# Self-attention of a fused attention block: value products four key blocks at a time instead of two

## The chip, the cores and the metric

The kernel runs on one core of a Trainium2 chip. The metric is the device time of one execution in microseconds (us); the time before is a median of 3 runs, 1094.27 us (1092.45 to 1095.04). The engines run side by side, each through its own list of instructions, and wait for each other by semaphores: PE (TensorE, matmuls and their weight loads), DVE (VectorE), ACT (ScalarE), POOL (GpSimd) and SP, which issues transfers. Matmul results land in PSUM, eight banks of 128 x 512 floats, and DVE or ACT copies them out.

## The reference

All is in float32, for x of 4 batches x 512 tokens x 160 channels. First an adapter layer (8 heads of 20) is applied. Then comes a block with three parts: self-attention with 20 heads of 64 over 512 tokens, cross-attention with 77 context tokens, and a feed-forward layer. The change is in the self-attention:

```python
x = cross_attention(layer_norm(x, g1, be1), layer_norm(x, g1, be1), wq1, wk1, wv1, wo1, bo1) + x

def cross_attention(x, ctx, wq, wk, wv, wo, bo):
    q, k, v = ...                                     # projections, 20 heads of 64
    scores = jnp.einsum('bhnd,bhmd->bhnm', q, k) * SCALE
    attn = jax.nn.softmax(scores, axis=-1)
    out = jnp.einsum('bhnm,bhmd->bhnd', attn, v)
    out = out.transpose(0, 2, 1, 3).reshape(B, N, HEADS * DHEAD)
    return jnp.einsum('bnf,fe->bne', out, wo) + bo
```

## The kernel before

The self-attention (`selfattn`, from L280) handles two heads at a time, a pair j of 10 in each batch (64 + 64 rows fill the 128 partitions). A pair has four blocks of 128 queries or keys. A unit u = 4j + q is one such block, 40 in a batch, and the program of every engine is written out over double units d, 20 in a batch, two units in each. The order of the instructions on each engine is the order of the code; nothing reorders it but the waits.

For a unit PE makes the scores of both heads (L388, six matmuls for a unit, as the product is made of three parts for each head) into a double bank. DVE takes the negated row maxima (L577), ACT the exponentials with their sums (L505, two per unit), DVE the reciprocals (L581), POOL scales the probabilities (L645). When all four units of a pair are scaled, PE transposes them by key block (`turns`, L402: eight transposes for a unit, four for each head e into the bank `b_turn[e]`). DVE copies the bank of head 0 (L586) and ACT that of head 1 (L516) into the SBUF tile `turned`, which has two buffers, u % 2. Each bank is single: the transposes of the next unit wait until the copy of their bank is done (L400). Then PE makes the value products (`pv`, L415): for each key block k of a pair two matmuls, one per head, which the profile records as four; each has 64 columns of weights, 512 moving columns and accumulates over k = 0..3 in one bank, `b_out`. After the fourth ACT copies this to `att` (L511), and at the end of a batch PE projects it out (`project_out`, L422), and DVE adds it to x (L594).

PE's order in double unit d (L444 to L466): the value products of units 2d-2 and 2d-1; in an even d the value projection (L232 to L235) of the pair after the next; the norm's transposes in d = 11 and 13; the transposes of unit 2d; the key projection (even d) or query projection (odd d), L224 to L227; the transposes of unit 2d+1; the scores of units 2d+6 and 2d+7, which may belong to the next batch. Behind d = 19 come the value products of units 38 and 39 and the output projection; d = 0 has no value products.

ACT's order (L529 to L546): the rounding of the next norm's output in d = 15 (L198 to L201); the exponentials of units 2d+4 and 2d+5, those whose scores PE made at the end of the double unit before, with the norm's scaling between them in d = 11 and 13 (L181, L186); in an even d the copy of the attention output (L511); the copy of transposed unit 2d; the rounding of k or q (L497, L493); the copy of unit 2d+1. DVE's order (L613 to L633): both maxima, a reciprocal, the copy of v in an even d (L573), the copy of unit 2d, a reciprocal, the copy of unit 2d+1, the remainder of k or q (L568, L563), and the norm's statistics behind d = 6 (L135, L139) and its standardizing behind d = 7 (L153).

A copy into `turned` waits for the transposes and for the value products that read that buffer last, s_pv of unit u-2.

Of the kernel before, what the change touches and what calls it, by code (L numbers as in the profile page):

```python
# [25 lines left out]
B, S, D = 4, 512, 160  # L26
P = 128
QT = S // P
# [30 lines left out]
def over_batches(eng, body):  # L59

    for b in range(B):
        body(b, b < B - 1)
# [217 lines left out]
def selfattn(nc, block, x, ident, ln, next_ln, w_q, w_k, w_v, w_o, bias_o, banks):  # L280

    NU = NPAIR * QT
# [16 lines left out]
    with ExitStack() as ctx:  # L299
        sb = lambda n, s, d=F32: ctx.enter_context(nc.sbuf_tensor("sa_" + n, s, d))  # L300
# [2 lines left out]
        k_parts = sb("k_parts", [P, 2, 2, S], F32R)  # L303
        v = sb("v", [P, 3, QT, 2 * P])
        probs = sb("probs", [P, 2, 2, QT, S])
        turned = sb("turned", [P, 2, 2, S])
        att = sb("att", [P, NPAIR, S])
        negmax = sb("negmax", [P, RING, 2])
        total = sb("total", [P, RING, 2])
# [2 lines left out]
        b_scores, b_turn, b_out, b_proj = [banks.pair(0), banks.pair(2)], banks[4:6], banks[6], banks[7]  # L312
# [16 lines left out]
        s_evac = sig("turned_copied", NU, 2)  # L329
        s_evac_act = sig("turned_copied_act", NU, 2)  # L330
        s_pv = sig("pv_made", NU, 6 * QT)
# [5 lines left out]
        def following(b, more):  # L337

            return (ln, b + 1, b + 1) if more else (next_ln, b + 1, 0)

        def wait_turned_copied(eng, b, u, e):

            s = s_evac_act if e == 1 else s_evac
            eng.wait_ge(s.sem, s.at(b, u))


        @block.tensor
        def _(pe):
            for s in (s_q, s_k, s_v, s_scores, s_turn, s_pv, s_o):
                pe.sem_inc(s.sem, s.credit)  # L350

            def project_q(b, j, bank=b_proj):
                ln.project(pe, bank, w_q, j * P).then_inc(s_q.sem, 1)

            def project_k(b, j, bank=b_proj):
                ln.project(pe, bank, w_k, j * P).then_inc(s_k.sem, 1)

            def project_v(b, j, bank=b_proj):
                for t in range(2):
                    last = ln.project_tokens(pe, bank[:, t * 2 * P:(t + 1) * 2 * P], w_v, j // 2 * 2 * P, j % 2 * 2 + t, 2 * P)  # L360
                last.then_inc(s_v.sem, 1)

            def next_q(b, j):
                if j == 0:
                    ln.ready(pe, b)
                pe.wait_ge(s_klo.sem, s_klo.at(b, j - 1))
                project_q(b, j)

            def next_v(b, j):
                pe.wait_ge(s_qlo.sem, s_qlo.at(b, j))  # L370
                project_v(b, j)

            def next_k(b, j):
                pe.wait_ge(s_vsb.sem, s_vsb.at(b, j))
                project_k(b, j)

            def scores(b, u):

                j, q = divmod(u, QT)
                if q == 0:  # L380
                    pe.wait_ge(s_qlo.sem, s_qlo.at(b, j))
                    pe.wait_ge(s_klo.sem, s_klo.at(b, j))
                pe.wait_ge(s_exp.sem, s_exp.at(b, 2 * u - 3))
                bank = b_scores[u % 2]
                for i, (a, c) in enumerate(((0, 0), (1, 0), (0, 1))):
                    for e in range(2):
                        rows = slice(e * HD, (e + 1) * HD)
                        last = pe.matmul(bank[:, e, :], q_parts[rows, j % 2, a, q * P:(q + 1) * P], k_parts[rows, j % 2, c, :],  # L388
                                         start=(i == 0), stop=(i == 2))
                last.then_inc(s_scores.sem, 1)  # L390

            def turns(b, u):

                j, k = divmod(u, QT)
                if k == 0:
                    pe.wait_ge(s_norm.sem, s_norm.at(b, 2 * QT * j + 2 * QT - 1))
                for e in range(2):
                    if u == 0:
                        pe.wait_ge(s_x.sem, s_x.at(b, e - 2))
                    wait_turned_copied(pe, b, u - 1, e)  # L400
                    for q in range(QT):
                        last = pe.transpose(b_turn[e][:, q * P:(q + 1) * P], probs[:, j % 2, e, q, k * P:(k + 1) * P], ident[:])  # L402
                    last.then_inc(s_turn.sem, 1)

            def pv(b, u):

                j, k = divmod(u, QT)
                for e in range(2):
                    wait_turned_copied(pe, b, u, e)
                if k == 0:  # L410
                    pe.wait_ge(s_vsb.sem, s_vsb.at(b, j | 1))
                    pe.wait_ge(s_att.sem, s_att.at(b, j - 1))
                for e in range(2):
                    c = j % 2 * P + e * HD
                    last = pe.matmul(b_out[e * HD:(e + 1) * HD, :], v[:, V_BUF[j // 2], k, c:c + HD],  # L415
                                     turned[:, u % 2, e, :], start=(k == 0), stop=(k == QT - 1))
                last.then_inc(s_pv.sem, 1)

            def project_out(q, first, end):

                for j in range(first, end):
                    last = pe.matmul(b_turn[q // 2][:, q % 2 * D:(q % 2 + 1) * D], att[:, j, q * P:(q + 1) * P],  # L422
                                     w_o[:, j, :], start=(j == 0), stop=(j == NPAIR - 1))
                return last

            ln.ready(pe, 0)
            project_q(0, 0, b_proj)
            project_k(0, 0, b_out)
            project_q(0, 1, b_turn[0])
            project_k(0, 1, b_turn[1])  # L430
            scores(0, 0)
            scores(0, 1)
            project_v(0, 0, b_proj)
            pe.wait_ge(s_klo.sem, s_klo.at(0, 0))
            project_v(0, 1, b_out)
            for u in range(2, 2 * LEAD):
                scores(0, u)
            project_q(0, 2, b_turn[0])
            for u in range(2 * LEAD, 2 * LEAD + 2):
                scores(0, u)  # L440
            pe.wait_ge(s_qlo.sem, s_qlo.at(0, 2))

            def batch(b, more):
                for d in range(ND):  # L444
                    norm, _, nb = following(b, more)
                    if d >= 1:
                        pv(b, 2 * d - 2)
                        pv(b, 2 * d - 1)
                    if d % 2 == 0:
                        over(next_v, b, d // 2 + 2, NPAIR, more)  # L450
                    if d == TURN_MAIN:
                        norm.turn_main(pe, nb, ident, b_proj, lambda: pe.wait_ge(s_klo.sem, s_klo.at(b, d // 2 + 2)))
                    if d == TURN_TAIL:
                        norm.turn_tail(pe, nb, ident, b_proj, lambda: pe.wait_ge(s_klo.sem, s_klo.at(b, d // 2 + 2)))
                    turns(b, 2 * d)
                    if d == TURN_MAIN:
                        pe.wait_ge(norm.s_full.sem, norm.s_full.at(norm.before + nb, 0))
                    if d == TURN_TAIL:
                        pe.wait_ge(norm.s_full.sem, norm.s_full.at(norm.before + nb, 1))
                    if d % 2 == 0:  # L460
                        over(next_k, b, d // 2 + 2, NPAIR, more)
                    else:
                        over(next_q, b, d // 2 + 3, NPAIR, more)
                    turns(b, 2 * d + 1)
                    for i in range(2):
                        over(scores, b, 2 * (d + LEAD + 1) + i, NU, more)  # L466

                pv(b, NU - 2)
                pv(b, NU - 1)
                project_out(0, 0, NPAIR - 1)  # L470
                pe.wait_ge(s_att.sem, s_att.at(b, NPAIR - 1))
                project_out(0, NPAIR - 1, NPAIR)
                for q in range(1, QT):
                    last = project_out(q, 0, NPAIR)
                    if q % 2 == 1:
                        last.then_inc(s_o.sem, 1)

            over_batches(pe, batch)

        @block.scalar  # L480
        def _(act):
# [30 lines left out]

            def copy_turned(b, u):
                act.wait_ge(s_turn.sem, s_turn.at(b, 2 * u + 1))
                act.wait_ge(s_pv.sem, s_pv.at(b, u - 2))
                act.copy(turned[:, u % 2, 1, :], b_turn[1]).then_inc(s_evac_act.sem, 1)  # L516

            round_q(0, 0, b_proj)
            round_k(0, 0, b_out)
# [32 lines left out]
        def _(dve):  # L552
# [29 lines left out]

            def copy_turned(b, u):
                dve.wait_ge(s_turn.sem, s_turn.at(b, 2 * u))
                dve.wait_ge(s_pv.sem, s_pv.at(b, u - 2))
                dve.tensor_copy(turned[:, u % 2, 0, :], b_turn[0]).then_inc(s_evac.sem, 1)  # L586

            def update(b):
                for half in range(2):
# [1324 lines left out]
```

## Time and profile before

| what | value |
| --- | --- |
| median of 3 runs | 1094.27 us |
| span of the profiled execution, first to last instruction | 1096.6 us |
| PE busy | 1018.4 us, 93% |
| DVE, ACT, POOL busy | 64%, 55%, 32% |
| mean granted TensorE clock | 0.964 of 2.4 GHz |
| value products L415 | 640 records, 155.0 us |
| transposes L402 | 1280 records, 175.1 us |

The profile is of one execution, and its span is what the rows below add up to; it lies 2.3 us above the median of the timed runs. The adapter fills the first 220 us or so, the self-attention runs to about 848 us, the cross-attention to about 1030 us, the feed-forward to the end. In a row "x8" is the number of records merged in it, and "[0.34 <-DVE sa_turned L586]" is idle time of the engine just before, with what ended it. Matmuls overlap, so their mean time is more than their distance.

### The profile page before, as it was taken

What the parts mean: (1) busy time and instruction counts of PE and PEld (TensorE: products, weight loads), DVE (VectorE), ACT (ScalarE), POOL (GpSimd) and SP (SyncE); (2) the same over time, 40 slices, a digit from 0 to 9 for tenths busy, and PEclk for the clock granted to TensorE, in tenths of its full rate; (3) what the DMA queues carried; (4) which work ended last, traced back from release to release, by engine and by line L of the source; (5) the groups of instructions that cost most, each with busy time, mean ns of one, the idle gap of its engine ahead of it and who ended that gap; (6) DMA issues with size and microseconds to landing.
All of it is one profiled execution on the core that took longest, in us unless ns stands there. A gap on an engine that the chain in (4) does not pass through costs nothing.

```text
span 1096.6 us, 17611 instructions
## 1 busy us (share of the span) xinstructions
PE 1018.4 (93%) x6388; PEld 721.8 (66%) x6388; DVE 706.5 (64%) x1228; ACT 598.1 (55%) x1344; POOL 350.0 (32%) x461
## 2 busy tenths in 40 slices
PE   6788887799999999999999999999999989999998
PEld 3455553556666766666766666766656569999887
DVE  2544737377767467767367767377662879999563
ACT  2534434466677456677366676366662654555432
POOL 2303214133433224433233433133331023444220
PEclk9878988899999999999999999999999999999999
DMA  6700000000000000000000000000000240000000
GB/s 165 186 1 1 2 1 0 1 1 1 1 1 1 1 1 2 1 1 1 1 1 1 1 1 1 1 1 1 1 1 1 64 129 14 1 1 1 1 25 25
DMA packets 25319, 17.67 MB, mean 16 GB/s; under 512 B 8482, under 2 KB 24050, under 8 KB 25234
## 3 DMA queue, kind: packets, MB, share of 16 engines
q1 hardware_dynamic: 25234, 16.54, 5.8%
q8 instruction: 52, 0.85, 0.3%
q14 instruction: 33, 0.27, 0.1%
HBM read 11.29 MB, written 1.31 MB: 11 GB/s over the span
## 4 chain that ended last, share of the span: by engine, by line
PE 61%; DVE 10%; ACT 5%; issue 4%; POOL 1%; DMA 0%; SPq 0%; DVEq 0%; ACTq 0%; POOLq 0%
PE banks L415 12%; PE banks L402 11%; PE banks L388 10%; PE banks L422 4%; ACT sa_probs L505 3%; PE banks L224 3%; PE banks L226 2%; PE banks L227 2%; PE banks L225 2%; PE banks L1460 2%; PE banks L1752 2%; DVE sa_negmax L577 2%; DVE ca_top L1595 1%; DVE ca_probs L1600 1%; PE banks L232 1%
## 5 line engine op out<-in xcount | busy, mean ns | idle before, releaser
L645 POOL TENSOR_SCALAR sa_probs<-sa_probs,sa_inverse 128x512 f32<-128x512 f32 x320 | 217.6, 696 | 373.8 <-DVE sa_inverse L581 373.7
L505 ACT ACTIVATE sa_probs<-banks,sa_negmax 128x512 f32<-128x512 f32 x320 | 215.9, 685 | 163.2 <-DVE sa_negmax L577 163.1
L577 DVE TENSOR_REDUCE sa_negmax<-banks 128x2 f32<-128x1024 f32 x160 | 188.6, 1218 | 12.6 <-PE banks L388 9.9
L402 PE MATMUL banks<-ident,sa_probs 128*128 128x128 f32 x1280 | 175.1, 278 | 10.0 <-ACT sa_turned L516 5.7
L402 PEld LDWEIGHTS banks<-ident,sa_probs 128*128 128x128 f32 x1280 | 146.9, 142 | 55.9 <-issue 28.0
L586 DVE COPY sa_turned<-banks 128x512 f32<-128x512 f32 x160 | 110.1, 688 | 77.5 <-PE banks L402 77.5
L415 PE MATMUL banks<-sa_turned,sa_v 128*64 128x512 f32 x640 | 155.0, 605 | 0.0
L388 PE MATMUL banks<-sa_k_parts,sa_q_parts 64*128 64x512 f32 x960 | 134.4, 411 | 1.9 <-ACT sa_probs L505 1.9
L516 ACT COPY sa_turned<-banks 128x512 f32<-128x512 f32 x160 | 94.4, 590 | 31.7 <-PE banks L402 30.0
L388 PEld LDWEIGHTS banks<-sa_k_parts,sa_q_parts 64*128 64x128 f32 x960 | 84.8, 187 | 31.2 <-issue 14.6
L415 PEld LDWEIGHTS banks<-sa_turned,sa_v 128*64 128x64 f32 x640 | 38.7, 136 | 74.2 <-issue 73.0
L1677 POOL TENSOR_TENSOR ca_probs<-ca_probs,ca_inverse 128x770 f32<-128x770 f32 x32 | 48.2, 1509 | 99.6 <-DVE ca_inverse L1606 99.6
L1460 PE MATMUL banks<-fold_values,ca_turned 119*128 119x160 f32 (+1 forms) x416 | 65.9, 303 | 2.1 <-ACT ca_turned L1539 1.5
L505 ACT ACTIVATION_READ_ACCUMULATOR sa_probs<-banks,sa_negmax 128x1 f32 x320 | 64.5, 202 | 0.0
L1460 PEld LDWEIGHTS banks<-fold_values,ca_turned 119*128 119x128 f32 (+1 forms) x416 | 59.6, 193 | 3.5 <-issue 2.7
L581 DVE RECIPROCAL sa_inverse<-sa_total 128x2 f32<-128x2 f32 x160 | 26.1, 163 | 48.7 <-ACT sa_probs L505 48.7
L1529 ACT ACTIVATE ca_probs<-ca_probs 128x770 f32<-128x770 f32 x32 | 27.0, 847 | 35.2 <-DVE ca_probs L1600 35.1
L422 PEld LDWEIGHTS banks<-w_o,sa_att 128*128 128x128 f32 x320 | 43.6, 190 | 3.2 <-issue 3.2
L1539 ACT COPY ca_turned<-banks 119x512 f32<-119x512 f32 x64 | 30.3, 500 | 27.6 <-PE banks L1448 27.6
L422 PE MATMUL banks<-w_o,sa_att 128*128 128x160 f32 x320 | 44.5, 300 | 0.0
L573 DVE COPY sa_v<-banks 128x512 f32<-128x512 f32 x40 | 27.5, 690 | 25.0 <-PE banks L235 25.0
L224 PE MATMUL banks<-ln_y_hi,wb_hi 128*128 128x512 f32 x80 | 36.6, 458 | 6.7 <-DVE sa_v L573 6.5
(212 smaller groups left out, 1757.4 us busy)
## 6 DMA issues: line engine op xcount, KB each, us to landing
w_o<-in_L_xattn_wo SPq DMA_DIRECT2D x2, 800.0 KB, 6.4
out<-x SPq DMA_DIRECT2D x4, 320.0 KB, 2.4
w_q_t<-in_L_xattn_wq_t SPq DMA_DIRECT2D x1, 1120.0 KB, 11.2
fold_values<-ca_turned SPq DMA_DIRECT2D x5, 192.5 KB
x<-in_x SPq DMA_DIRECT2D x1, 960.0 KB, 6.0
fold_values<-ca_probs SPq DMA_DIRECT2D x4, 192.5 KB
ad_raw_main<-in_L_xattn_wq SPq DMA_DIRECT2D x1, 640.0 KB, 4.1
ad_raw_main<-in_L_xattn_wk SPq DMA_DIRECT2D x1, 640.0 KB, 6.2
```

Source lines behind the costliest of these rows:

```text
L224: pe.matmul(bank, w.hi[:, c], self.hi[:], start=True, stop=False)
L388: last = pe.matmul(bank[:, e, :], q_parts[rows, j % 2, a, q * P:(q + 1) * P], k_parts[rows, j % 2, c, :], start=(i == 0), stop=(i == 2))
L402: last = pe.transpose(b_turn[e][:, q * P:(q + 1) * P], probs[:, j % 2, e, q, k * P:(k + 1) * P], ident[:])
L415: last = pe.matmul(b_out[e * HD:(e + 1) * HD, :], v[:, V_BUF[j // 2], k, c:c + HD], turned[:, u % 2, e, :], start=(k == 0), stop=(k == QT ...
L422: last = pe.matmul(b_turn[q // 2][:, q % 2 * D:(q % 2 + 1) * D], att[:, j, q * P:(q + 1) * P], w_o[:, j, :], start=(j == 0), stop=(j == NP ...
L505: act.activation(probs[:, j % 2, e, q, :], b_scores[u % 2][:, e, :], ACT.Exp, bias=negmax[:, u % RING, e:e + 1], accum_out=total[:, u % RI ...
L516: act.copy(turned[:, u % 2, 1, :], b_turn[1]).then_inc(s_evac_act.sem, 1)
L577: dve.tensor_reduce(negmax[:, u % RING, :], b_scores[u % 2], AX_X, ALU.max, negate=True).then_inc(s_max.sem, 1)
L586: dve.tensor_copy(turned[:, u % 2, 0, :], b_turn[0]).then_inc(s_evac.sem, 1)
L645: pool.tensor_scalar(probs[:, j % 2, e, q, :], probs[:, j % 2, e, q, :], inverse[:, u % RING, e:e + 1], 1.0, ALU.mult, ALU.mult).then_inc( ...
L1460: last = pe.matmul(b_out[t % 2][:, 0:D], turned[0:w, i, :], folded.values[0:w, t // QT, i, :], start=(i == 0), stop=(i == folded.TILES - 1))
L1677: pool.tensor_tensor(p, p, inverse[:, t % RING, u, :].unsqueeze(2).broadcast_to([P, HH, SK]), ALU.mult).then_inc(s_norm.sem, 1)
```

## The change

PE no longer makes the value products of two units in each double unit. It makes all four of a pair, in a row, in each second double unit: at the head of d = 2, 4, ... 18 and behind d = 19. In an odd d the transposes of unit 2d follow right on the scores. The transposed probabilities get four buffers (one per key block) in place of two, and the copies into them wait for the value products of unit u-4 in place of u-2. The number of instructions that compute is the same.

```diff
-        turned = sb("turned", [P, 2, 2, S])
+        turned = sb("turned", [P, QT, 2, S])
...
                     last = pe.matmul(b_out[e * HD:(e + 1) * HD, :], v[:, V_BUF[j // 2], k, c:c + HD],
-                                     turned[:, u % 2, e, :], start=(k == 0), stop=(k == QT - 1))
+                                     turned[:, k, e, :], start=(k == 0), stop=(k == QT - 1))
...
-                    if d >= 1:
-                        pv(b, 2 * d - 2)
-                        pv(b, 2 * d - 1)
+                    if d % 2 == 0 and d > 0:
+                        for k in range(QT):
+                            pv(b, 2 * d - QT + k)
...
-                pv(b, NU - 2)
-                pv(b, NU - 1)
+                for k in range(QT):
+                    pv(b, NU - QT + k)
...
             def copy_turned(b, u):
                 act.wait_ge(s_turn.sem, s_turn.at(b, 2 * u + 1))
-                act.wait_ge(s_pv.sem, s_pv.at(b, u - 2))
-                act.copy(turned[:, u % 2, 1, :], b_turn[1]).then_inc(s_evac_act.sem, 1)
+                act.wait_ge(s_pv.sem, s_pv.at(b, u - QT))
+                act.copy(turned[:, u % QT, 1, :], b_turn[1]).then_inc(s_evac_act.sem, 1)
...
                 dve.wait_ge(s_turn.sem, s_turn.at(b, 2 * u))
-                dve.wait_ge(s_pv.sem, s_pv.at(b, u - 2))
-                dve.tensor_copy(turned[:, u % 2, 0, :], b_turn[0]).then_inc(s_evac.sem, 1)
+                dve.wait_ge(s_pv.sem, s_pv.at(b, u - QT))
+                dve.tensor_copy(turned[:, u % QT, 0, :], b_turn[0]).then_inc(s_evac.sem, 1)
```

## Rows read from the trace of the kernel before

**Rows 1.** The page, part 1: busy time, share of the span, instructions.

```profile
PE 1018.4 (93%) x6388; PEld 721.8 (66%) x6388; DVE 706.5 (64%) x1228; ACT 598.1 (55%) x1344; POOL 350.0 (32%) x461
```

**Rows 2.** The page, part 5, a group: after the bar busy us, mean ns, idle before.

```profile
L505 ACT ACTIVATE sa_probs<-banks,sa_negmax 128x512 f32<-128x512 f32 x320 | 215.9, 685 | 163.2 <-DVE sa_negmax L577 163.1
```

**Rows 3.** Two stretches: length, busy PE, PEld, DVE, ACT, POOL, granted clock, DMA, GB/s.

```profile
507.95:514.24 6.29, 6.29 (x42) 3.97 (x41) 4.67 (x8) 4.44 (x11) 2.35 (x5) 1.00 0.00 0
514.24:521.71 7.47, 7.47 (x49) 5.00 (x48) 5.16 (x9) 5.03 (x12) 3.09 (x5) 1.00 0.01 2
```

**Rows 4.** Timeline of PE, an odd double unit: start us, length us, engine, what.

```profile
521.71 1.65 PE L388 MATMUL banks<-sa_k_parts,sa_q_parts 64*128 64x512 f32 x12
523.29 1.94 PE L415 MATMUL banks<-sa_turned,sa_v 128*64 128x512 f32 x8
525.16 1.09 PE L402 MATMUL banks<-ident,sa_probs 128*128 128x128 f32 x8
526.01 0.48 PE L224 MATMUL banks<-ln_y_hi,wa_hi 128*128 128x512 f32 x1
...
527.03 1.04 PE L402 MATMUL banks<-ident,sa_probs 128*128 128x128 f32 x8
528.00 0.50 PE L388 MATMUL banks<-sa_k_parts,sa_q_parts 64*128 64x512 f32 x2
```

**Rows 5.** Timeline of the same odd double unit, DVE and ACT.

```profile
522.72 2.36 DVE L577 TENSOR_REDUCE sa_negmax<-banks 128x2 f32<-128x1024 f32 x2
...
523.98 0.69 ACT L505 ACTIVATE sa_probs<-banks,sa_negmax 128x512 f32<-128x512 f32 x1 [1.57 <-DVE sa_negmax L577]
...
526.64 0.60 ACT L516 COPY sa_turned<-banks 128x512 f32<-128x512 f32 x1
```

**Rows 6.** Timeline, weight loads of the value products in that unit.

```profile
523.78 0.14 PEld L415 LDWEIGHTS banks<-sa_turned,sa_v 128*64 128x64 f32 x2 [0.29 <-issue]
...
524.21 0.14 PEld L415 LDWEIGHTS banks<-sa_turned,sa_v 128*64 128x64 f32 x2 [0.29 <-issue]
```

**Rows 7.** Timeline of the last batch, double units 16 and 17.

```profile
818.65 0.60 ACT L511 COPY sa_att<-banks 128x512 f32<-128x512 f32 x1
...
819.79 0.66 PE L402 MATMUL banks<-ident,sa_probs 128*128 128x128 f32 x4 [0.52 <-ACT sa_turned L516]
...
820.38 1.66 PE L388 MATMUL banks<-sa_k_parts,sa_q_parts 64*128 64x512 f32 x12
...
825.27 1.34 PE L402 MATMUL banks<-ident,sa_probs 128*128 128x128 f32 x8 [0.34 <-DVE sa_turned L586]
...
826.54 1.94 PE L415 MATMUL banks<-sa_turned,sa_v 128*64 128x512 f32 x8
```

**Rows 8.** Timeline of double unit 7, behind the statistics of the norm.

```profile
434.79 1.66 PE L388 MATMUL banks<-sa_k_parts,sa_q_parts 64*128 64x512 f32 x12
...
441.65 0.66 PE L402 MATMUL banks<-ident,sa_probs 128*128 128x128 f32 x4 [0.36 <-ACT sa_turned L516]
```

**Rows 9.** Timeline of double unit 11, with the norm's scaling on ACT.

```profile
463.46 1.66 PE L388 MATMUL banks<-sa_k_parts,sa_q_parts 64*128 64x512 f32 x12
...
467.62 0.78 ACT L181 ACTIVATE ln_full<-banks,be,g 128x512 f32<-128x512 f32 x1 [0.44 <-PE banks L161]
...
470.26 0.66 PE L402 MATMUL banks<-ident,sa_probs 128*128 128x128 f32 x4 [0.19 <-ACT sa_turned L516]
```

**Rows 10.** Timeline of double unit 15, with the norm's rounding.

```profile
493.10 1.66 PE L388 MATMUL banks<-sa_k_parts,sa_q_parts 64*128 64x512 f32 x12
...
499.91 0.66 PE L402 MATMUL banks<-ident,sa_probs 128*128 128x128 f32 x4 [0.64 <-ACT sa_turned L516]
```

**Rows 11.** Timeline at the start of a batch: the projections before and after a wait.

```profile
546.59 0.50 PE L224 MATMUL banks<-ln_y_hi,wb_hi 128*128 128x512 f32 x1 [2.17 <-DVE sa_v L573]
```

**Rows 12.** Stretches around that wait, and the last batch's double unit 15: columns as rows 3.

```profile
546.58:551.70 5.12, 5.11 (x24) 3.82 (x24) 2.51 (x5) 2.15 (x5) 2.25 (x4) 0.67 0.01 2
806.32:813.72 7.40, 5.80 (x37) 3.23 (x36) 6.12 (x10) 5.60 (x13) 2.26 (x5) 1.00 0.00 1
```

## The prediction

> **What bounds the kernel now.** I read the page's busy shares first: TensorE (PE) is busy 93% of the span [rows 1], no other engine over 64%. A share is an average, so I then read the self-attention on the timeline. A double unit is called here by the stretch that its scores open: stretch d runs from the scores that PE issues at the end of double unit d-1 to those at the end of d; S is its first instant. Odd stretches take 6.29 us and even ones 7.47 us in the middle of a batch, and PE is busy in all of both [rows 3]. So a pair of heads costs 13.76 us, and the bound there is PE.
>
> But look how little is behind it. In an odd stretch (S = 521.71) PE goes through scores for 1.58 us, value products for 1.87, the first transposes for 0.85, a query projection for 1.02, the second transposes for 0.97 [rows 4]. Beside it runs a chain that the same scores start: VectorE (DVE) starts its maxima at S+1.01, ScalarE (ACT) its four exponentials at S+2.27, and only behind them in ACT's order comes the copy that empties the second transpose bank, at S+4.93 to S+5.53 [rows 5]. The second half of the second transposes needs that bank. PE gets there about S+5.8 (half of the 0.97 us before the end), so the chain is late by less than 0.3 us of becoming the bound. ACT's 163 us of idling on maxima [rows 2] say the same: it has the time, but its work can't start before the scores are there.
>
> Where PE has less to do, the chain shows. In the last batch's stretch 17 there is no projection: its value products and transposes are all PE has, yet it lasts 820.38 to 826.54 = 6.16 us, with a wait of 0.34 us for DVE's copy and then one for ACT's [rows 7]. By rows 5 and one more number, the 0.59 us from the late transposes to the next scores (819.79 to 820.38) [rows 7], the chain gives 5.53 + 0.59 = 6.12 us and a hand-over, for which the 6.16 us leave 0.04. Both agree: no stretch with exponentials in this order can be shorter than 6.16 us, whatever PE's work is.
>
> **The change, part by part.** It moves the value products of two units (1.87 us) out of each odd stretch into the following even one (for stretch 19: behind it, ahead of the output projection). No instruction is added or taken away: still 640 value products, the same copies, no DMA, no engine queue but PE's reordered.
>
> *Even stretches.* Eight matmuls more stand in one row with eight of their kind. Their pace is 0.43 us for two (weight loads at 523.78 and 524.21) [rows 6], so eight add 4 x 0.43 = 1.72 us; the group alone takes 1.87 [rows 4], and the 0.15 us between are its entry and exit, paid once now. PE is the bound there without a gap [rows 3], so all 1.72 us are on the path: 7.47 becomes 9.19. Queued behind them are the value projection, transposes and key projection; DVE's and ACT's copies of these keep their distance to PE. The copy of the attention output on ACT waits for the last product, at about S+5.3 where it used to go at S+4.93; ACT then still has its copy of the transposes done before PE, at S+8.1, wants the bank. Cost nothing; with that cover gone it would be at most the 0.4 us of delay. There are 10 such places in each batch (stretches 2, 4 to 18, and the end), 40 in all: 40 x 1.72 = +68.8 us. In the last batch's stretch 16 PE already waits 0.52 us for ACT, which there copies the attention output first [rows 7], and no projections are left, so part of the added work hides: -0.9 us by the same bookkeeping.
>
> *Odd stretches.* PE is ready for the second half of the second transposes at S+1.58+0.85+1.02+0.48 = S+3.9, give or take 0.3 for what the change from scores straight to transposes costs (not in the trace before; bounded by nothing and by the whole rest of the scores' 1.58 us). Either way it is far ahead of ACT, whose copy lets it go on at S+5.57. So the 1.87 us taken out don't shorten the stretch; they turn into waiting, and only 6.29 - 6.16 = 0.13 us is won. Six stretches in a batch are such (1, 3, 5, 9, 17, 19); without the last batch's 17 and 19, 22 in all: -2.9 us. Of the other four, 7 (DVE does the norm's statistics ahead of the maxima) and 15 (ACT rounds first) are bound by this chain already: PE waits 0.36 and 0.64 us for ACT's copy [rows 8, 10]. They stay as they are: 0. In 11 and 13 ACT waits 0.44 us for the norm's transposes, which stand behind the value products [rows 9]; these come earlier now and the wait goes: -0.5 us each, 8 in all, -4.0 us.
>
> *The four buffers.* A copy into them now waits for products four units back, made in the stretch before or at the head of this one. The reason that this costs nothing: in both cases PE has them behind it before it makes the transposes that are to be copied. Also 0: transposes right behind scores at the head of an odd stretch want DVE's and ACT's last copies, due at S+0.7, while PE arrives at S+1.58.
>
> *The clock.* Where PE waited 2.17 us at a batch's start [rows 11], the granted clock fell: 0.67 over the next 5.12 us, all busy, so part of it at 1.2 GHz [rows 12]. That cost 5.12 x 0.33 = 1.7 us. The new waits: an odd stretch's work is over at S+3.6 and the late transposes come at S+5.57, with one half of transposes (0.66 us) between: 5.57 - 3.6 - 0.66 = 1.3 us idle, in two pieces. In the last batch's stretch 15 PE is idle 1.6 of 7.40 us at a granted clock of 1.00 [rows 12], so I expect no fall from these. But in stretches 7 and 15 the late transposes come at S+6.86 and S+6.81 [rows 8, 10]: 6.8 - 3.6 - 0.66 = 2.6 us idle, as much as at the batch's start. That is 8 places; bounds are none (0) and every one at full price (8 x 1.7 = 13.6). A fall partly spent in waiting costs less and not each gap need cause one, so I take 40%: +5.5 us.
>
> *Sum*: 68.8 - 0.9 - 2.9 - 4.0 + 5.5 = +66.5 us, or about +1.6 us for each of 40 head pairs. The profiled execution's span is 1096.6 us, 2.3 above the median of 1094.27; the sum is small beside this, so I add it to the median: 1161 us.
>
> **The rule that speaks for the change.** The 0.15 us of entry and exit of a value group are what rows 4 and 6 show of switching. The Trainium skill (TensorEngine Tiling (Array Packing), Key Properties) says that changing the tiling mode drains TensorE; scores (64 rows), value products (64 columns) and transposes (whole array) are three modes, and the change saves one passage in each pair. By that rule alone the kernel would get faster. The trace agrees that a passage costs something, but in an odd stretch PE waits anyway.
>
> **Rivals.** *PE stays the bound (the other side: faster).* If ACT's copy came in time, PE's work alone would count: 40 groups fewer at 0.15 us each (6 us), up to 0.45 us if the way into value products also costs 0.3 more than the way into transposes (18 us): 1076 to 1088, say 1082 us. The point from which it decides: ACT's copy must be done by S+4, against S+5.53. For it: PE at 93%. Against: the chain hangs on the scores and nothing in the change starts them earlier; stretch 17 shows it bare [rows 7].
>
> *The clock falls in all odd stretches.* If 1.3 us idle in two pieces is enough, some 24 further stretches lose 1.7 us at about every second chance: +20 us more, 1182 us. Against it: 1.6 us idle at full clock [rows 12]. The Trainium skill (TensorE: Matmul & The Clock Gate, A second HAM failure mode) tells of small idle gaps between groups that make the clock swing; stretch 15 of the last batch doesn't bear it out.
>
> *Half of it hidden, or nothing moves.* If the waits were absorbed over several stretches, say because DVE or ACT start ahead after the long even ones, +30 us: 1125 us. Against: ACT idles before its first exponential, 1.57 us on maxima [rows 5], so there is nothing to catch up.
>
> **How the numbers follow.** Forecast 0.86 (1161 us), clock 0.06, hidden 0.03, PE-bound 0.05. The forecast's own range is 61 (no clock falls) to 75 us more, 1155 to 1169; with the clock price and small errors in 40-fold terms (0.1 us each is 4 us) the range is 1151 to 1172. What this kernel's measurement can tell from no change is about 0.2%, 2 us; slower by more than that 0.93, faster 0.05, within it 0.02.
>
> **What would show it.** Right: L388 starts 6.16 us apart in odd and 9.19 in even stretches; L402 shows idle time before it for DVE's L586 (about 1 us) and ACT's L516 (some 0.4 us) in every odd stretch, 45 to 60 us in all; ACT's idling on L577 does not fall; value products come 16 in a row. Clock falls behind the gaps of stretches 7 and 15. Wrong: odd stretches of about 4.5 us, or even ones under 9 us; a pair that sums to under 13.76 would overturn the whole argument.

## The result and the profile after

The changed kernel takes 1163.07 us in the median of 4 runs (1157.46 to 1166.32) against 1093.36 us (1091.99 to 1095.04): a ratio of 1.064 (1.060 to 1.067), 69.7 us slower. The forecast was 1161 us. The profiled execution spans 1164.4 us, 67.8 more than that of before.

The page of the changed kernel, its rows that answer to [rows 1, 2]; in the PE row of part 2 a digit is the busy tenths of one of 40 slices:

```profile
span 1164.4 us, 17611 instructions
...
PE 1036.7 (89%) x6388; PEld 730.0 (63%) x6388; DVE 705.7 (61%) x1228; ACT 600.0 (52%) x1344; POOL 349.6 (30%) x461
...
PE   6798888888998898999898999898988998999998
...
L505 ACT ACTIVATE sa_probs<-banks,sa_negmax 128x512 f32<-128x512 f32 x320 | 215.9, 686 | 166.2 <-DVE sa_negmax L577 166.1
L402 PE MATMUL banks<-ident,sa_probs 128*128 128x128 f32 x1280 | 187.1, 286 | 49.5 <-DVE sa_turned L586 38.5
...
L415 PE MATMUL banks<-sa_turned,sa_v 128*64 128x512 f32 x640 | 148.0, 605 | 0.0
```

PE is busy 18 us more but in a span 68 us longer, and the share falls from 93 to 89%: most of the time went into PE's waiting. The group L402 says for whom: before the transposes PE is idle for 49.5 us, most of it for DVE's copy. In the page of before that is 10.0 us:

```profile
L402 PE MATMUL banks<-ident,sa_probs 128*128 128x128 f32 x1280 | 175.1, 278 | 10.0 <-ACT sa_turned L516 5.7
```

ACT's idling on the maxima has not fallen (166.1 against 163.1 us), so nothing runs ahead.

Four stretches of the changed kernel, columns as in [rows 3]: a plain odd one, the even one behind it, then stretches 15 and 16:

```profile
538.05:544.22 6.17, 4.86 (x33) 3.38 (x32) 5.04 (x9) 4.35 (x11) 2.23 (x5) 1.00 0.00 0
544.22:553.38 9.16, 9.16 (x57) 5.58 (x56) 4.79 (x8) 5.13 (x12) 3.20 (x5) 1.00 0.01 2
520.47:528.32 7.85, 5.88 (x33) 3.89 (x32) 6.77 (x11) 6.10 (x14) 2.71 (x5) 0.86 0.00 1
528.32:538.05 9.73, 9.73 (x57) 6.02 (x56) 4.34 (x8) 5.14 (x12) 2.73 (x5) 0.94 0.00 0
```

The odd stretch lasts 6.17 us with PE busy 4.86; the even one 9.16 and busy throughout. The pair is 15.3 us, where it was 13.76 [rows 3]. In stretch 15 the granted clock is 0.86 and behind it 0.94.

The timeline of that odd stretch, which answers to [rows 4, 5]; S is 538.05:

```profile
538.05 1.66 PE L388 MATMUL banks<-sa_k_parts,sa_q_parts 64*128 64x512 f32 x12
...
539.06 2.35 DVE L577 TENSOR_REDUCE sa_negmax<-banks 128x2 f32<-128x1024 f32 x2
...
539.65 1.09 PE L402 MATMUL banks<-ident,sa_probs 128*128 128x128 f32 x8
540.32 0.69 ACT L505 ACTIVATE sa_probs<-banks,sa_negmax 128x512 f32<-128x512 f32 x1 [1.57 <-DVE sa_negmax L577]
...
540.49 0.47 PE L224 MATMUL banks<-ln_y_hi,wa_hi 128*128 128x512 f32 x1
...
541.88 0.69 DVE L586 COPY sa_turned<-banks 128x512 f32<-128x512 f32 x1
...
542.62 0.66 PE L402 MATMUL banks<-ident,sa_probs 128*128 128x128 f32 x4 [0.95 <-DVE sa_turned L586]
...
542.99 0.60 ACT L516 COPY sa_turned<-banks 128x512 f32<-128x512 f32 x1
...
543.64 0.66 PE L402 MATMUL banks<-ident,sa_probs 128*128 128x128 f32 x4 [0.36 <-ACT sa_turned L516]
...
544.22 1.64 PE L388 MATMUL banks<-sa_k_parts,sa_q_parts 64*128 64x512 f32 x12
...
545.79 0.20 PEld L415 LDWEIGHTS banks<-sa_turned,sa_v 128*64 128x64 f32 x4 [0.35 <-issue]
```

Transposes follow the scores after 1.60 us, the projection after 2.44. Its four matmuls are over at S+3.6. The chain is where it was: maxima at S+1.01, first exponential at S+2.27, ACT's copy at S+4.94. PE gets the first bank (head 0, DVE's copy) at S+4.57, the second (head 1, ACT's copy) at S+5.59, and the next scores start at S+6.17. The four units of value products behind it:

```profile
545.79 3.65 PE L415 MATMUL banks<-sa_turned,sa_v 128*64 128x512 f32 x16
549.38 0.39 PE L232 MATMUL banks<-wc_hi,ln_y_hi 128*128 128x256 f32 x1
```

16 matmuls in 3.59 us, against 8 in 1.87 [rows 4]: 1.72 us more, as eight at 0.43 us for two.

### The profile page after: what moved, and what is told of

Read it like the earlier page. It is cut to its first block, busy times and chain, and to the rows that moved or that the text cites. A ratio compares the mean times of both kernels' runs of the same rounds, so it can differ in the third digit from the quotient of the medians.

```text
span 1164.4 us, 17611 instructions
## 1 busy us (share of the span) xinstructions
PE 1036.7 (89%) x6388; PEld 730.0 (63%) x6388; DVE 705.7 (61%) x1228; ACT 600.0 (52%) x1344; POOL 349.6 (30%) x461
## 4 chain that ended last, share of the span: by engine, by line
PE 53%; DVE 13%; ACT 10%; issue 4%; POOL 1%; DMA 0%; SPq 0%; ACTq 0%; DVEq 0%; POOLq 0%
PE banks L415 12%; PE banks L402 9%; PE banks L388 9%; ACT sa_probs L505 8%; DVE sa_negmax L577 5%; PE banks L422 4%; PE banks L224 2%; PE banks L1460 2%; PE banks L1752 2%; PE banks L227 2%; PE banks L225 2%; PE banks L226 2%; ACT sa_turned L516 1%; DVE ca_top L1595 1%; DVE ca_probs L1600 1%
## 5 line engine op out<-in xcount | busy, mean ns | idle before, releaser
L505 ACT ACTIVATE sa_probs<-banks,sa_negmax 128x512 f32<-128x512 f32 x320 | 215.9, 686 | 166.2 <-DVE sa_negmax L577 166.1
L402 PE MATMUL banks<-ident,sa_probs 128*128 128x128 f32 x1280 | 187.1, 286 | 49.5 <-DVE sa_turned L586 38.5
L402 PEld LDWEIGHTS banks<-ident,sa_probs 128*128 128x128 f32 x1280 | 148.5, 145 | 93.3 <-DVE sa_turned L586 52.7
L577 DVE TENSOR_REDUCE sa_negmax<-banks 128x2 f32<-128x1024 f32 x160 | 188.7, 1218 | 23.9 <-PE banks L388 21.9
L415 PE MATMUL banks<-sa_turned,sa_v 128*64 128x512 f32 x640 | 148.0, 605 | 0.0
L388 PE MATMUL banks<-sa_k_parts,sa_q_parts 64*128 64x512 f32 x960 | 139.5, 423 | 1.9 <-ACT sa_probs L505 1.9
L388 PEld LDWEIGHTS banks<-sa_k_parts,sa_q_parts 64*128 64x128 f32 x960 | 88.8, 196 | 33.4 <-issue 15.7
L415 PEld LDWEIGHTS banks<-sa_turned,sa_v 128*64 128x64 f32 x640 | 42.9, 138 | 84.3 <-issue 84.0
```

Source lines behind the costliest of these rows:

```text
L505: act.activation(probs[:, j % 2, e, q, :], b_scores[u % 2][:, e, :], ACT.Exp, bias=negmax[:, u % RING, e:e + 1], accum_out=total[:, u % RI ...
L577: dve.tensor_reduce(negmax[:, u % RING, :], b_scores[u % 2], AX_X, ALU.max, negate=True).then_inc(s_max.sem, 1)
```

## The experiments

The kernel before was timed again beside the experiments: its medians were 1094.5 us beside experiments 1 to 4, 1095.1 beside 5 to 7 and 1093.3 beside 8, and each ratio is to the one of its own occasion. Where an experiment is set against the changed kernel (1163.07 us), the two were timed on different occasions. In the edits the engine whose list is changed is named where it isn't PE.

**1. Only stretches 7 and 15 as before.**

```diff
+                    if d in (7, 15):
+                        pv(b, 2 * d - 2)
+                        pv(b, 2 * d - 1)
                     if d % 2 == 0 and d > 0:
-                        for k in range(QT):
+                        for k in range(2 if d in (8, 16) else 0, QT):
```

> The changed kernel, but in stretches 7 and 15 of each batch the two value products stay where they were before the change (and stretches 8 and 16 make only the other two). Theory (a stretch lasts as long as the longer of PE's work and ACT's chain; PE's long waits in 7 and 15 drop the clock): stretches 7 and 15 stay at 7.4 us as the chain rules them, 8 and 16 go from 9.19 to 7.47, so 8 places x 1.72 = 14 us less, and the clock no longer falls behind 7 and 15 (7 falls at about 1 us each), another 7 us: about 1142 us. Rival (the clock falls cost nothing or have another cause): only 14 us less, 1149, and the falls stay. Rival (PE is the bound everywhere, grouping itself is what costs): the time goes by groups, 4 fifths of the loss stay, 1149.

Measured: 1141.6 us (1133.85 to 1141.92), ratio 1.041 (1.036 to 1.046), 21.5 us under the changed kernel. Stretches 15 and 16 of it:

```profile
514.86:522.25 7.39, 6.73 (x41) 3.88 (x41) 6.22 (x11) 6.10 (x14) 2.24 (x5) 1.00 0.01 2
522.25:529.71 7.46, 7.46 (x49) 5.00 (x48) 4.79 (x8) 5.02 (x12) 3.19 (x5) 1.00 0.00 1
```

Stretch 15 takes 7.39 us, as before the change (7.40), and has its value products back at no cost; stretch 16 takes 7.46 us, and the clock is at 1.00 in both. It fell nowhere in this profile's self-attention. The theory's 21 us are there; the rivals said 14. Summed over stretches 7, 8, 15 and 16 of the four batches, the profile is 21.9 us under the changed kernel's. Another 4.7 us of it are at the three batch starts, where the clock didn't fall either; that was not part of the theory.

**2. The group of four in the odd stretches.**

```diff
-        turned = sb("turned", [P, QT, 2, S])
+        turned = sb("turned", [P, 6, 2, S])
...
-                    if d % 2 == 0 and d > 0:
+                    if d % 2 == 1 and d > 1:
                         for k in range(QT):
-                            pv(b, 2 * d - QT + k)
+                            pv(b, 2 * d - QT - 2 + k)
@@ ACT @@
-                    if d % 2 == 0 and d > 0:
+                    if d % 2 == 1 and d > 1:
                         copy_att(b, d // 2 - 1)
@@ DVE @@
                     over(maxima, b, m + 1, NU, more)
-                    over(inverses, b, m, NU, more)
                     if d % 2 == 0:
                         over(copy_v, b, d // 2 + 2, NPAIR, more)
-                    copy_turned(b, 2 * d)
+                        copy_turned(b, 2 * d)
+                        over(inverses, b, m, NU, more)
+                    else:
+                        over(inverses, b, m, NU, more)
+                        copy_turned(b, 2 * d)
```

(Not shown: the indices of the six buffers, (b * NU + u) % 6, with waits for unit u-6, and of the three buffers of v, which now turn through all batches, (5 b + j // 2) % 3, as the products come later.)

> The same four products in a row, but at the head of the odd stretches (3, 5, ... 19, and one group behind 19), in which PE had less other work and which ACT's chain rules in 7, 11, 13 and 15; six buffers for the turned probabilities, the copy of the attention output moved with them, and in even stretches DVE copies v and the turned block ahead of the reciprocal. Theory: odd stretches 6.29 + 1.72 = 8.01 us, PE-bound; even ones without value products ruled by the wait for DVE's copies, 6.1 to 6.2 us (up to 6.6); a plain pair 14.1 to 14.2 against 13.76 before and 15.36 in the changed kernel, and in the pairs with 7, 11, 13, 15 a gain of 0.2 to 0.8 against before: together 1092 to 1102 us. Rival (four products in a row cost by themselves, or by PE's clock): as the changed kernel, about 1160 us.

Measured: 1106.8 us (1104.52 to 1115.42), ratio 1.013 (1.008 to 1.019): 56 us under the changed kernel with the same four products in a row, 5 us over the range given. A plain odd stretch and the even one behind it:

```profile
417.64:425.64 8.00, 8.00 (x50) 4.54 (x49) 4.42 (x8) 5.14 (x12) 3.89 (x7) 1.00 0.00 1
425.64:431.81 6.17, 5.84 (x41) 4.50 (x41) 5.22 (x9) 4.33 (x11) 1.52 (x3) 1.00 0.00 0
```

8.00 + 6.17 = 14.17 us, as worked out. What was missed stands mainly in stretches 11 and 13, 9.6 and 9.5 us, where the expectation left room for 8.5 at most: the norm's scaling on ACT now waits for transposes that stand behind four value products, and everything behind it in ACT's order waits with it. Stretch 8 takes 7.12 us too, as PE waits 1.28 us for DVE's copy of v, behind the norm's standardizing and the maxima. ACT in stretch 11 (S = 461.10):

```profile
466.97 0.78 ACT L181 ACTIVATE ln_full<-banks,be,g 128x512 f32<-128x512 f32 x1 [2.16 <-PE banks L161]
...
468.97 0.59 ACT L511 COPY sa_att<-banks 128x512 f32<-128x512 f32 x1
```

**3. The changed kernel with the copies earlier.**

```diff
@@ ACT @@
+                    if d % 2 == 1:
+                        copy_turned(b, 2 * d)
                     over(exps, b, 2 * (d + LEAD) + 1, NU, more)
...
-                    copy_turned(b, 2 * d)
+                    if not (d % 2 == 1):
+                        copy_turned(b, 2 * d)
@@ DVE @@
+                    if d % 2 == 1:
+                        copy_turned(b, 2 * d)
                     over(maxima, b, m + 1, NU, more)
...
                     if d % 2 == 0:
                         over(copy_v, b, d // 2 + 2, NPAIR, more)
-                    copy_turned(b, 2 * d)
+                        copy_turned(b, 2 * d)
```

> The changed kernel; in odd double units ACT copies the first transposed unit between the two units' exponentials instead of behind both, and DVE copies it between the two maxima. Theory: PE gets the bank at S+4.25 instead of S+5.57, odd stretches fall from 6.17 to about 4.85 us (24 plain ones: 32 us less), 7 and 15 by about 1.3 and 11 and 13 by 0.5 us (14 us), and the clock falls of 7 and 15 go (7 us): about 1110 us, still over before, since 9.19 + 4.85 = 14.04. If the delayed exponentials hold up the next scores, up to 5.5 us and 1130. Rival (the odd stretches are long for another reason, not ACT's copy): no change, 1160.

Measured: 1112.0 us (1106.56 to 1112.22), ratio 1.015 (1.011 to 1.019). PE in a plain odd stretch:

```profile
410.59 1.65 PE L388 MATMUL banks<-sa_k_parts,sa_q_parts 64*128 64x512 f32 x12
412.17 1.09 PE L402 MATMUL banks<-ident,sa_probs 128*128 128x128 f32 x8
...
414.04 0.60 PE L402 MATMUL banks<-ident,sa_probs 128*128 128x128 f32 x4
414.83 0.66 PE L402 MATMUL banks<-ident,sa_probs 128*128 128x128 f32 x4 [0.19 <-ACT sa_turned L516]
415.41 0.96 PE L388 MATMUL banks<-sa_k_parts,sa_q_parts 64*128 64x512 f32 x6
```

410.59 to 415.41 = 4.82 us. Only two engines' order of copies was changed, PE's order is that of the changed kernel; 51 us of its 70 come back. What is left is in the main what two unequal stretches still waste: 9.30 + 4.82 = 14.1 us for a plain pair, against 13.76.

**4. The kernel before with the early copy in 11, 13 and 15** (on ACT alone, the condition is `d in (11, 13, 15)`).

> The kernel before; only in double units 11, 13 and 15 ACT copies the first transposed unit between the two units' exponentials. Theory: these three are ruled by ACT's copy already (7.39, 7.31, 7.40 us), and PE's own work there is 6.75, 6.75 and 6.29 us; gain 0.45 + 0.45 + 1.1 = 2.0 us in each batch, 8 us in all: 1085 us. Rival (PE's work, not the copy, sets them): nothing, 1093.

Measured: 1083.07 us (1081.93 to 1084.72), ratio 0.990 (0.986 to 0.993), faster than both kernels. The three stretches last 6.99, 6.93 and 6.54 us, where 7.39, 7.31 and 7.40 stood. That is 6.5 us in four batches, somewhat less than the 8 expected. Another 3.1 us between the two profiles are clock falls at two of the three batch starts, which this profile hasn't; so the agreement of the medians (1083 for 1085) is in part luck. Stretch 15:

```profile
486.45:492.99 6.54, 6.52 (x42) 3.92 (x41) 5.35 (x8) 5.62 (x14) 1.53 (x3) 1.00 0.01 3
```

**5. More PE work in odd stretches**, in the changed kernel and in the one before:

```diff
                 pe.wait_ge(s_klo.sem, s_klo.at(b, j - 1))
+                ln.project(pe, b_proj, w_q, j * P)
                 project_q(b, j)
```

> The changed kernel with more PE work: each query projection of the running part of the self-attention is made twice (the second overwrites the first in the same bank), four matmuls or 0.95 us more in each odd stretch. Theory: PE waits 1.3 us there, so plain odd stretches stay at 6.17 us; 7 and 15 stay at 7.45 and 7.40 and their gap shrinks from 2.6 to 1.6 us, so that the clock falls behind them go (about 7 us less); 11 and 13, where the projection starts late, grow by about 0.5 us each (4 us): about 1160 us, within 5 of the changed kernel. Rival (PE is the bound in the changed kernel too, its loss is in slower value products or mode changes): 37 x 0.95 = 35 us more, 1198 us.

> The kernel before with the same doubled query projections. Theory: plain odd stretches are PE-bound and go from 6.29 to 7.25 us, 22 x 0.96 = 21 us; 7 and 15 stay under their chain (0), 11 and 13 grow by about 0.6 each, 5 us: 26 us more, about 1119 us. Rival (the kernel before is ruled by the chain as well): under 5 us more.

Measured: 1156.92 us (1156.38 to 1159.37), ratio 1.056 (1.053 to 1.059), and 1117.22 us (1116.16 to 1117.95), ratio 1.019 (1.016 to 1.022). The same work makes the kernel before 22 us slower and doesn't slow the changed one: its median is 6 us less. An odd stretch of the kernel before with it, then PE in one of the changed kernel:

```profile
409.39:416.60 7.21, 7.21 (x45) 4.73 (x44) 4.67 (x8) 4.45 (x11) 2.88 (x5) 1.00 0.01 2
```


```profile
434.61 1.65 PE L389 MATMUL banks<-sa_k_parts,sa_q_parts 64*128 64x512 f32 x12
...
438.05 0.40 PE L224 MATMUL banks<-ln_y_hi,wa_hi 128*128 128x512 f32 x1
...
439.17 0.66 PE L403 MATMUL banks<-ident,sa_probs 128*128 128x128 f32 x4
440.19 0.66 PE L403 MATMUL banks<-ident,sa_probs 128*128 128x128 f32 x4 [0.35 <-ACT sa_turned L517]
440.77 1.66 PE L389 MATMUL banks<-sa_k_parts,sa_q_parts 64*128 64x512 f32 x12
```

In the kernel before, the stretch grows from 6.29 to 7.21 us. In the changed one there are four matmuls more (from 438.05) and it still takes 6.16 us; the 0.95 us came out of the waiting. Stretches 7 and 15 last 7.44 and 7.39 us, as in the kernel before, and the clock fell only once with them in the profile, in the last batch's 15, which has no projection to double. Against the profile of the changed kernel this is 6.3 us less in stretches 7, 8, 15 and 16, and 1.6 us less at the batch starts, where one fall didn't come; stretches 11 and 13 are 4.3 us more, as expected. So the time won is that of the falls.

**6. More ACT work in odd stretches of the kernel before.**

```diff
+                    if d % 2 == 1:
+                        act.wait_ge(s_spare.sem, s_spare.at(b, d // 2 - 1))
+                        act.copy(spare[:], w_o[:, 0:3, :]).then_inc(s_spare.sem, 1)
                     copy_turned(b, 2 * d)
```

> The kernel before with one more copy of 480 columns (about 0.56 us) on ACT in each odd double unit, right ahead of the copy of its first transposed unit; it computes nothing that is used. Theory: the chain ends 0.13 us before PE's work in plain odd stretches, so 0.56 us more on it lengthens them by 0.43 us, to 6.72 (22 x 0.43 = 10 us), and those that it rules (7, 11, 13, 15) by 0.56 each (9 us): about 19 us more, 1112 us. Rival (PE-bound with slack on the other engines, as the busy shares of 93 and 55% suggest): nothing, 1093 us.

Measured: 1112.53 us (2 runs, 1111.65 and 1113.41), ratio 1.015 (1.011 to 1.019). Its plain odd stretch:

```profile
425.83:432.49 6.66, 6.50 (x41) 3.96 (x41) 5.04 (x9) 4.84 (x12) 2.72 (x5) 1.00 0.00 0
```

6.66 us: ACT is busy 4.84 us of it and yet sets it. The copy moves what is behind it by 0.48 us rather than 0.56, and of this 0.48 - 0.13 = 0.35 us should show; 0.37 do. Stretches 7, 11, 13 and 15, which the chain ruled already, grew by the whole of it, 0.48 to 0.50 us. So the kernel before stood 0.13 us from its second bound.

**7. The four buffers alone**, in the order of before.

> The order of before with the four buffers of the change alone. Theory: the copies never waited for value products, so the time of before, within 2 us of 1093. Rival (the larger tile or its addresses cost something, or the buffers alone free the copies): more than 2 us either way.

Measured: 1092.77 us (8 runs, 1090.71 to 1099.3), ratio 0.999 (0.996 to 1.002). The self-attention takes 583.4 us in this profile and in that of before, from the first scores of stretch 1 to those of stretch 17 of the last batch. The buffers do nothing by themselves; the medians differ by 2.4 us, but within their spread.

**8. The batch's start too.** To experiment 4 is added:

```diff
@@ DVE @@
                     over(inverses, b, m, NU, more)
+                    if d == 0 and b > 0:
+                        update(b - 1)
...
-                update(b)
+                if not more:
+                    update(b)
```

> The kernel before with the early copy in double units 11, 13 and 15, and DVE's adding of the output projection to x (which stands ahead of the next batch's maxima) moved behind the maxima and reciprocal of that batch's double unit 0. Theory: the maxima, exponentials and copies of double unit 0 then run beside the 11 us of output projection, and the wait of 2.17 us for DVE's copy of v at each of three batch starts goes, with the clock falls behind it (0 to 1.6 us each): 7 to 11 us less than the early copy alone, 1072 to 1076 us. Rival (that wait is set by PE's own value projection): as the early copy alone, 1083.

Measured: 1078.56 us (1074.40 to 1080.72), ratio 0.987 (0.983 to 0.990), the fastest version by its median. DVE's copy of v and the key projection that waited 2.17 us for it [rows 11]:

```profile
378.68 0.69 DVE L576 COPY sa_v<-banks 128x512 f32<-128x512 f32 x1 [0.46 <-PE banks L235]
...
379.42 0.50 PE L224 MATMUL banks<-ln_y_hi,wb_hi 128*128 128x512 f32 x1
```

The wait is gone, and scores follow scores over a batch's end after 18.34 us each time, against 20.60 in experiment 4 where the clock held and 22.16 where it fell. Against experiment 4, which ran on another occasion, the medians differ by 4.5 us, less than the 7 to 11 expected; the profiled self-attentions do differ by 8.3 us (573.9 and 565.5 us over the same stretches), so what is missing lies outside it or in the spread of the runs. That is left open.

To this the early copies of double unit 7 were then added, on ACT and on DVE:

> As e10_early_update, with the early copies of double unit 7 on ACT and DVE too. Theory: stretch 7 falls from 7.44 to 6.3 to 6.5 us, but what ACT puts off (the rounding of q, the second copy) and DVE's standardizing behind it delay the maxima of stretch 8, which lasts 7.47 by PE with only about half a us of slack: stretch 8 grows to 8 to 8.7. Together between 4 us less and 1 us more than e10_early_update; I expect 1 to 2 us less.

Measured: 1080.05 us (5 runs, 1074.08 to 1082.16), ratio 0.988 (0.984 to 0.991), no different from the kernel without them; the 1 to 2 us less that were expected didn't come. Stretch 7 fell from 7.44 to 6.31 us and stretch 8 grew from 7.47 to 8.74, in one batch to 8.90: a stall handed on to the next stretch.

## Why the prediction was right

From the first scores of stretch 1 (236.47) to those of stretch 17 of the last batch (886.25) the changed kernel takes 649.8 us, the one before 583.4: 66.4 us of the 67.8 between the spans. In that part lie 38 of the 40 groups. The split by terms is worked out from the lengths of the stretches:

| term | predicted (on these stretches) | measured, summed over the stretches |
| --- | --- | --- |
| two more units in 38 places | 38 x 1.72 = +65.4 | +65.2 |
| hidden in the last batch's stretch 16 | -0.9 | -0.7 |
| plain odd stretches, 22 | -2.9 | -2.5 |
| stretches 11 and 13 | -4.0 | -4.3 |
| clock falls behind 7 and 15 | +5.5 | +8.8 |
| sum | +63.1 | +66.4 |

Outside it the two last groups should have added 3.4 us, and the spans differ by 1.4. So two misses, +3.3 us in the clock's term and -2.0 us outside, cancel in part: that the sum, 66.5 us, lies within 1.3 us of the spans' 67.8 is better than its terms. The mechanism stands in the stretches themselves.

*The even stretches.* 9.19 was forecast, 9.16 to 9.19 stand there. ACT's copy of the attention output waits 0.2 us for the products, and PE waits for nothing in that stretch. In the last batch's stretch 16 what follows the value products takes 2.47 us (883.78 to 886.25) where it took 3.20 (817.18 to 820.38): these are the 0.7 us hidden.

*The odd stretches.* 6.16 was forecast, 6.17 measured. That a chain and not PE's work sets them is shown from three sides: with the copies earlier in the chain they are shorter (experiment 3), more PE work doesn't lengthen them (5), and where the value products stand decides what they cost (1 and 2). In stretches 11 and 13 ACT's wait for the norm's transposes is gone, as forecast. That the group of four itself costs is refuted by experiment 2.

*The clock.* This was the one term that was mis-sized, +5.5 us for +8.8. I took 40% of 8 falls at 1.7 us; 7 of the 8 came. Six cost about 1.05 us each (stretches 15 and 16: 7.85 + 9.73 against 7.40 + 9.18). A part passes in waiting: stretch 7 idles 2.59 us in the batch without a fall and 2.2 in the others. The last batch's cost 2.6 us; it came behind the longest gap, 2.83 us, and the granted clock of its stretch 16 is 0.76, where 0.94 stands for the others. That makes 8.8 us in all. Experiments 1 and 5 took falls away and left stretches 7 and 15 at the forecast 7.4 us.

The idling ahead of the falls was not the 2.6 us of the forecast. In stretch 7 it was 2.23 us in one piece. In stretch 15 PE waits 0.97 us before the projection, whose input ACT and DVE have just rounded, and 0.70 us for DVE's copy, and there the clock falls, at 526.15:

```profile
520.47:526.15 5.68, 4.01 (x27) 2.75 (x27) 5.35 (x8) 4.53 (x11) 0.79 (x2) 1.00 0.00 0
526.15:528.32 2.17, 1.87 (x8) 1.14 (x7) 1.42 (x3) 1.58 (x4) 1.92 (x4) 0.50 0.01 4
```

So 1.7 us in two pieces came before it. The forecast had excused the plain odd stretches with the last batch's stretch 15, 1.6 us idle in two pieces at full clock [rows 12]. That is a weak reason: the kernel before of experiment 5 has the same pieces there, 0.96 and 0.64 us, and a fall right behind them:

```profile
823.88:831.27 7.39, 5.79 (x37) 3.23 (x37) 6.11 (x10) 5.60 (x13) 2.26 (x5) 1.00 0.02 3
831.27:838.76 7.49, 7.14 (x37) 3.85 (x36) 3.71 (x6) 4.44 (x11) 2.81 (x5) 0.77 0.00 0
```

The plain odd stretches, idle 1.3 us, did lose none, as said; the row of before didn't show that they would not.

*The rule on tiling modes.* The way from scores into transposes is no shorter than into value products: 1.60 us (538.05 to 539.65) and 1.57 (544.22 to 545.79). What fewer groups save is the 0.15 us once in each pair, 6 us in all; it is why an even stretch grew by 1.72 and not by 1.87. The Trainium skill (TensorEngine Tiling (Array Packing), Key Properties) says that changing the tiling mode drains TensorE. The 0.15 us would fit that, but no run here separates such a drain from other costs at the ends of a group; whatever it is, it is too small here to matter.

## What to carry to other kernels

Each stretch of an engine's list lasts as long as the longer of two things: the engine's own work in it, and the chain on other engines that it must wait for. Taking work out of a stretch shortens it only down to the chain; putting it into a stretch whose own work is the longer costs all of it. Before regrouping, take from the trace for each stretch both numbers, the work and the time when the last wait for another engine ends, and sum the larger ones. A stretch that waits is also where an edit in the order of another engine pays: here one copy moved between two exponentials took 6.5 us off, while a group of matmuls that "saved" 6 us cost 70.

## What the runs showed of the hardware

A gap of the same length didn't always bring the clock down. In the changed kernel PE idled 2.23 us in one piece in stretch 7 of every batch; in three the clock fell, in the first not (7.44 us there and 9.19 behind it). At the batches' starts the gap is 2.17 us with either order: it was followed by a fall at all three in the kernel before, at one in experiment 4 and at none in experiment 1. 1.6 us in two pieces, in the last batch's stretch 15, were followed by none in the kernel before and by one in its variant of experiment 5.

With a fall the stretches 0 and 1 took together 30.05 us in the changed kernel, without one 28.47 in experiment 1: 1.6 us, near the 1.7 read from [rows 12]. What decides whether a fall comes, stays open.
